# Count blocks of a graph kernel: one per pair of node blocks at fixed places, and one per tile for what runs over

## The reference

```
def _fa_layer(h, row, col, Wt_l, bt_l, Wg_l, bg_l):
    h = h @ Wt_l.T + bt_l
...
    g = jnp.tanh(h[row] @ Wg_l + bg_l)
    norm = g * dinv[row] * dinv[col]
    msg = norm[:, None] * h[row]
    out = jax.ops.segment_sum(msg, col, num_segments=n)
    return out + h
```

## Time and profile before

| | |
|---|---|
| median of three executions | 3942.78 us (3939.83 to 3947.1) |
| the profiled execution's own time | 3943.99 us |
| its span, first to last instruction | 3942.1 us |
| busy: PE, PEld | 2308.3, 2029.6 us |
| busy: DVE, ACT, POOL | 2210.6, 1280.8, 2021.6 us |
| mean granted clock of TensorE | 0.743 |

### The profile page before, as it was taken

The page is one execution under the profiler, slowest core; times in us unless marked ns, Lnnn a source line. Parts: engine busy times, 40 slices in busy tenths (PEclk is TensorE's granted clock), DMA queues, the critical chain, the costliest instruction groups (busy, mean ns, idle before and its releaser), DMA issues.

```text
span 3942.1 us, 59800 instructions
## 1 busy us (share of the span) xinstructions
PE 2308.3 (59%) x15144; PEld 2029.6 (51%) x15171; DVE 2210.6 (56%) x5804; ACT 1280.8 (32%) x3481; POOL 2021.6 (51%) x2076
## 2 busy tenths in 40 slices
PE   5972223666655666756756545554556666676665
PEld 4971213555534555545656544454445555665565
DVE  8988916777763555553665565778775222132212
ACT  4210011333220333335777754777762000000000
POOL 2777777777747777735777744777750000000000
PEclk9985555666666665556565667778778999989999
DMA  2210001122131344433333324444441222212221
GB/s 81 68 40 4 4 20 58 53 53 52 53 50 52 117 126 124 130 73 89 81 81 81 80 31 123 129 131 131 131 83 59 75 74 80 74 54 75 79 74 53
DMA packets 151496, 298.20 MB, mean 76 GB/s; under 512 B 49862, under 2 KB 67579, under 8 KB 151091
## 3 DMA queue, kind: packets, MB, share of 16 engines
q0 software_dynamic: 72704, 138.94, 15.1%
q1 hardware_dynamic: 74214, 145.16, 11.7%
q10 hardware_dynamic: 4430, 12.43, 1.0%
HBM read 249.70 MB, written 46.67 MB: 75 GB/s over the span
## 4 chain that ended last, share of the span: by engine, by line
POOL 40%; PE 24%; issue 18%; DVE 11%; ACT 3%; DMA 2%; DVEq 1%; POOLq 0%; ACTq 0%; SPq 0%
POOL arena L710 18%; PE psum L1495 15%; POOL pool L710 13%; POOL rec_dram L687 7%; DVE pool L2118 4%; PE psum L1420 3%; PE psum L1225 2%; ACT pool L882 2%; POOL ACC L710 2%; DVE ACC L2338 1%; PE psum L1263 1%; PE psum L1449 1%; ACT pool L811 1%; PE psum L1100 1%; DVE pool L1717 1%
## 5 line engine op out<-in xcount | busy, mean ns | idle before, releaser
L710 POOL DMA_INDIRECT arena<-tab_dram,tblk x832 | 794.0, 954 | 409.1 <-issue 249.5
L1495 PE MATMUL psum<-arena,pool 128*128 x4096 | 568.7, 293 | 301.3 <-DVE pool L2118 293.8
L1495 PEld LDWEIGHTS psum<-arena,pool 128*128 128x128 f32 x4096 | 527.4, 189 | 343.3 <-issue 342.7
L2118 DVE CAST pool<-pool 128x1024 f32<-128x1024 bf16 x256 | 177.1, 694 | 673.4 <-PE psum L1495 672.8
L687 POOL DMA_INDIRECT rec_dram<-arena,ACC x400 | 395.2, 988 | 196.4 <-issue 119.2
L710 POOL DMA_INDIRECT pool<-tab_dram,arena x416 | 401.1, 964 | 131.4 <-issue 126.4
L1543 PE MATMUL psum<-pool 128*128 128x136 f32 (+1 forms) x1664 | 362.0, 399 | 80.2 <-DVE pool L2262 73.9
L1543 PEld LDWEIGHTS psum<-pool 128*128 128x128 f32 x1664 | 335.3, 290 | 92.4 <-issue 51.7
L1379 PE MATMUL psum<-pool 128*128 128x128 f32 x832 | 192.8, 425 | 294.0 <-DMA pool<-tab_dram,arena 200.4
L710 POOL DMA_INDIRECT pool<-tab_dram,tblk x272 | 277.8, 1021 | 126.3 <-issue 78.6
L1379 PEld LDWEIGHTS psum<-pool 128*128 128x128 f32 x832 | 179.8, 328 | 298.4 <-DVE pool L2131 132.3
(11 more groups left out here) (378 smaller groups left out, 4760.6 us busy)
## 6 DMA issues: line engine op xcount, KB each, us to landing
pool<-items_dram SPq DMA_DIRECT2D x128, 512.0 KB, 3.3
items_dram<-pool SPq DMA_DIRECT2D x128, 256.0 KB, 2.5
pool<-dst_dram SPq DMA_DIRECT2D x104, 256.0 KB, 3.5
arena<-tab_dram,tblk POOLq DMA_INDIRECT x832
HN<-in_edge_attr_dram ACTq DMA_DIRECT2D x23, 500.0 KB
pool<-tab_dram,arena POOLq DMA_INDIRECT x416
rec_dram<-arena,ACC POOLq DMA_INDIRECT x400, 2.1
pool<-tab_dram,tblk POOLq DMA_INDIRECT x272
```

The source lines that it names most:

```text
L710: nc.gpsimd.indirect_dma_start(to[:, j, :], None, tab_dram[k], bass.IndirectOffsetOnAxis(ap=idx[:, G * g + j:G * g + j + 1], axis=0)).then ...
L1495: last = nc.tensor.matmul(psum[:, bass.ds(vals[BITE + j] * P, P)], item, of, start=False, stop=False)
L2118: v.tensor_copy(bite32[slot % 4], bite16[slot]).then_inc(s_cast, 1)
```

## The change

The items get another order and another meaning. The first FIRSTS = 640 places are one for each pair of blocks (25 x 25 = 625, then 15 of padding): place 25 d + s holds the counts of destination block d and source block s in the first tile in which that pair occurs. The remaining 416 places are one for each tile: the counts of the source block that began in an earlier tile and runs on into this one. ITEMS becomes 1056, 132 packs.

In a block pass the first kind is multiplied at addresses that are constants of the program (padding is skipped but for one matmul); the second kind still reads its block numbers, 52 times 16 of them. The order of a pass is 52 rounds of one or two packs of the first kind and one of the second, written out without a loop, on TensorE, DVE and SyncE. There are six f32 buffers instead of four. Items are stored and loaded as bytes (U8) instead of bf16, one pack (128 KB) a DMA. The tables are worked out anew for this layout; packing begins at group 8; for the second kind the picks are no products but two DVE operations over all tiles in `item_tiles`, and the picks by product are 640 wide instead of 1024.

More of the change, by code:

```diff
@@ L48 @@
 C_FIELDS, C_PICKS = 4, 8
-ROWS_THERE = 65
+ROWS_THERE = 96
+FAR = 4096.0
 BIG = 1.0e30
@@ L355, in gnn_kernel @@
[L355 to L360, removed]
@@ L362, in gnn_kernel @@
+        fields = MT[:, 1216:1216 + 3 * TILES // 2].bitcast(BF16).rearrange("p (a t) -> p a t", a=3)
+        field_i = MT[:, 1216 + 3 * TILES // 2:1216 + 5 * TILES // 2].bitcast(I32)
+        ends = [MT[:, 1216 + ITEMS * i:1216 + ITEMS * (i + 1)].bitcast(BF16).rearrange("p (w a) -> p w a", a=2) for i in range(2)]
+        behind_row = pool2[0:1, 9216:9216 + FIRSTS // 2].bitcast(BF16)
         onehots = [[ZT[:, PACK * P * b + PACK * P // 2 * e:PACK * P * b + PACK * P // 2 * (e + 1)].bitcast(BF16) for e in range(2)] for b in range(PACKS_A_GROUP)]
-        packed = [FT[:, PACK * P // 2 * b:PACK * P // 2 * (b + 1)].bitcast(BF16) for b in range(PACKS_A_GROUP)]
@@ L364, in gnn_kernel @@
-        bite16 = [pool2[:, BITE * P // 2 * b:BITE * P // 2 * (b + 1)].bitcast(BF16) for b in range(LONG)]
-        bite32 = [pool2[:, BITE * P * b:BITE * P * (b + 1)] for b in range(4, 8)]
-        where = MT[0:1, 0:2 * ITEMS].bitcast(I32)
+        packed = [FT[:, PACK * P // 4 * b:PACK * P // 4 * (b + 1)].bitcast(U8) for b in range(PACKS_A_GROUP)]
+        bite8 = [pool2[:, PACK * P // 4 * b:PACK * P // 4 * (b + 1)].bitcast(U8) for b in range(LONG)]
+        bite32 = [pool2[:, 2048 + PACK * P * b:2048 + PACK * P * (b + 1)] for b in range(HELD)]
@@ L367, in gnn_kernel @@
+        where = MT[0:1, 0:2 * TILES].bitcast(I32)
         newblk = sb("newblk", [P, 2, SLOTS * H + 1])
@@ L1474, in turn_sums, with item_regs @@
                 last.then_inc(s_itemp, 1)
-            def item_regs(n):
+            def item_regs(q):
                 _, vals = nc.values_load_multi_w_load_instructions(
-                    where[0:1, bass.ds(2 * BITE * n, 2 * BITE)], engines=[pe.engine], min_val=0, max_val=NB - 1,
+                    where[0:1, 2 * G * q:2 * G * (q + 1)], engines=[pe.engine], min_val=0, max_val=NB - 1,
                     skip_runtime_bounds_check_because="the table holds block numbers of at most NB - 1")
@@ new lines, in _ @@
+            link(v.tensor_scalar(full_, tot[:, :], 0.0, None, ALU.is_gt))
+            link(v.tensor_copy(span_i, span[:, 0, :]))
+            link(v.tensor_single_scalar(span_i, span_i, 7, ALU.arith_shift_right))
+            link(v.tensor_copy(none_, span_i))
+            link(v.scalar_tensor_tensor(none_, none_, 1.0, full_, ALU.add, ALU.mult))
+            link(v.tensor_scalar(first_tile, none_[0:NB, :], -1.0, None, ALU.add))
+            link(v.tensor_scalar(none_, full_, -1.0, -FAR, ALU.add, ALU.mult))
@@ new lines, in _ @@
+            link(v.scalar_tensor_tensor(first_behind, iota[0:NB, 0:NB], -float(P), none_[0:NB, :], ALU.mult, ALU.subtract))
+            link(v.memset(pad_tile, -1.0))
+            link(v.memset(pad_behind, -FAR))
+            for a in range(2):
+                link(v.scalar_tensor_tensor(bucket4[:, a, 0:NB], none_, FAR, span[:, a, :], ALU.mult, ALU.add))
+            link(v.tensor_scalar(bucket4[:, 2, :], iota[:, 0:28], -float(P), FAR, ALU.mult, ALU.add))
+            link(v.tensor_copy(bucket4[:, 3, :], iota[:, 0:28]))
@@ L2092, in long_pass @@
                             item_tiles()
-                        elif 4 <= g < 4 + (PAIRS + 7) // 8:
-                            for c in range(2 * g - 8, min(2 * g - 6, (PAIRS + 3) // 4)):
+                        elif 3 <= g < 3 + (PAIRS + 7) // 8:
+                            for c in range(2 * g - 6, min(2 * g - 4, (PAIRS + 3) // 4)):
                                 edge_steps(c)
```

132 lines of the change are left out of this document (55 added, 77 removed).

## The result

The changed kernel takes 3550.22 us (median of four executions, 3546.99 to 3552.29); the kernel before took 3943.23 us (four executions) on the same chip. The ratio is 0.9002, with a 95% interval of 0.8987 to 0.9018. The profiled execution took 3552.29 us around a span of 3550.4 us.

The account below looks back on a forecast made before the run. It took TensorE's sequencer, with its reads and register addresses, to bound the block passes. 870.1 - 2 x 238.5 = 393 us off, 3 on, so 390; 3943.99 - 390 - 1.2 = 3553 us, own range 3535 to 3579, 8-in-10 range 3535 to 3610.

Parts of the forecast that it names:

- The bound (the sequencer and its reads): Block passes before: TensorE's sequencer, with a 1.10 us read per bite and register work per matmul, sets the pace, not L2118.
- A pass: Each block pass after the change: 231.3 + 3.6 + 3.6 = 238.5 us, where the two took 870.1 us.
- The array's rate: TensorE's array in a block pass: 0.111 us a pair at full clock, 2084 pairs, a floor of 231.3 us.
- The missed lead: In 24 rounds with one constant-address pack, the sequencer's lead falls some 0.15 us short each: 3.6 us a pass.
- The half clock at the start: Start of a block pass: the first 64 pairs take 10.70 us instead of 7.1, costing 3.6 us.
- The 12 pairs: TensorE's sequencer can be at least 12 pairs ahead of the array, read from the start of the first block pass.
- The second sum pass: Where blocks are packed: +3 us at its end; bounds untaken were 26 us for the byte copy, 9 us back from gathers.
- Exposed loads: Rival for the block passes: no lead builds and reads stay exposed, 305 us a pass, 3686 us; chance 0.12.
- The 0.123 us a pair for register addresses: Rival: constant addresses run no faster than register ones, 263.5 us a pass, 3603 us; chance 0.06.
- The cast: Rival: DVE's cast from bytes becomes the bound, 391 us a pass, 3858 us; chance 0.05, shared with another new wait.
- Code supply: Rival: in-line passes need about 36 instruction packets; slower than before only above 10.8 us standstill each; chance 0.02.

Follow-up runs that it names:

- e7: The changed kernel with two f32 buffers for cast packs instead of six: 3553.1 us, 237.1 us a pass.
- e4: The changed kernel with the 80 constant-address packs of a pass first and the 52 register-address packs last: 3696.2 us, 308.0 us a pass.
- e6: The changed kernel with register-address packs four at a time between constant-address ones: 3649.5 us, 287.3 us a pass.
- e10: The changed kernel with a read of block numbers in every pack, kept by one register-address matmul in each constant-address pack: ratio 0.942 to before, 283.8 us a pass.
- e5: The changed kernel with register-address packs two at a time between constant-address ones: 3606.6 us, 265.0 us a pass.
- e9: The changed kernel with each register-address pack reading its 16 block numbers twice: ratio 0.939 to before, 281.0 us a pass.
- e1: The kernel before with its block passes written out in line instead of looped, all matmuls still at register addresses: 3894.5 us, 408.9 us a pass.
- e11: The changed kernel with packs 0 to 77 as matmuls of 512 columns, 4 pairs instead of 16: ratio 0.918 to before, 229.5 us a pass.
- e3: The changed kernel with a read of block numbers added to every pack, unused, so absent from the program that ran: 3553.5 us, void.

## Why the prediction was right

The prediction was 3553 us and the kernel takes 3550.2; each term against its measure:

**The bound (the sequencer and its reads).** Right. The profile's name for the wait, the cast L2118, was wrong, as argued: e7 leaves the cast a third of its buffers and the time stays, while e4 to e6 only move packs and bring back the same [<-DVE] rows. The idle column named what came last by the records it has; the sequencer's own work has no such record, and one finds it by its instructions.

**A pass.** Forecast 231.3 + 3.6 + 3.6 = 238.5; measured 235.3 and 235.8. The array's rate was sized right: 2084 x 0.1117 = 232.8 (1.5 over). The missed lead, 3.6, is nothing but the last pack's 0.4. The half clock at the start is 1.7 (3.52 us for 16 pairs instead of 1.79), not 3.6: I had it last for all 64 pairs of the row. In before it lasted for 29 of them, up to 3027.4 us, and the last 16 went at the sequencer's pace.

The step on the missed lead failed. Its 0.15 us is 1.4 for the read less 1.25 rebuilt by one constant pack; it leaves out the 0.2 us that it says the register pack lost, and the 1.25 rests on 0.033 us for handing over a constant pair, where e10 has under 0.01. So a single constant pack fills the lead up again. The 12 pairs that it took as shown, 1.34 us, were a lower bound of a row, where the bound is 16. The read and the first addresses take 1.4 us and 16 pairs last 1.79, so there is no stall. The Trainium skill (Advanced Engine Details and Errata, section Engine Queue Depths) gives TensorE a queue of 64 instructions, 32 pairs. By it too the term falls away, but the runs disagree with its figure: by 32 pairs e5 would be at 235 us a pass and e9 at 246, and they are at 265 and 281. The lead here ends at 16 pairs, 32 instructions, all of f32 matmuls.

**The second sum pass.** Forecast +3. DVE gets past the last store at 1745.71 us (L1895), and at 1743.57 in before:

```profile
1745.71 2.48 DVE L1895 TENSOR_TENSOR pool<-psum,HN 128x512 f32<-128x512 f32 x4 [14.60 <-DMA items_dram<-pool]
```

The eight profiles with the new packing where before takes 3943 to 3949 us have 1743.0 to 1747.0, mean 1745.9; the two with the old have 1743.56 and 1743.57. So +2.3. The copy to bytes costs 597 ns, as the one to bf16, and the gathers keep their 1.30 us, so neither bound of that step came into play.

**What I hadn't seen.** The block passes start 4.7 us later than in before: 2.1 from there and 2.6 from the attention stages between, which the change doesn't touch. From the end of the second sum pass to the first block pass before and e1 have 1277.7 and 1279.9 us, after 1280.3 and the seven others 1279.5 to 1283.5; whether that is more than scatter is open. Between the two block passes, from the last weight load to the first, lie 37.3 us instead of 34.7, but 34.1 to 35.2 in the seven others and 36.9 in e11, so it looks like scatter from one execution to the next. The ledger of the profiled executions by their windows: -399.0 (passes) + 4.7 (ahead) + 2.5 (between) + 0.1 (behind) = -391.7, and 3550.4 - 3942.1 = -391.7. It comes close to the 390 forecast because 6 us too much in the passes and 4 us too little ahead of and between them partly cancel.

**The rivals.** Exposed loads: not in this order, but real. It is what the same packs cost in e4, and its 305 us a pass is e4's 308. Whether it happens hangs on a margin of 0.4 to 0.6 us per register pack. The 0.123 us a pair for register addresses: L1501 follows at 1.79 us a pack, as L1505, so it belonged to the sequencer. The cast: 694 ns from bytes, as from bf16. Code supply: the instruction queue moved 34 packets more over the kernel (90 against 56; forecast were 36), and no gap in the passes answers to them; its only trace may be e1's slips, which the lead covers in after.

## What to carry to other kernels

Where TensorE has gaps and the profile names a producer that was long done, add up the sequencer's side: here 1.16 us for a read of 16 numbers, 0.245 us for each matmul at register addresses, under 0.01 us a pair at constant ones, against 0.1117 us a pair of the array. If part of the work can have constant addresses, that is not enough: it has to lie between the rest, so that each read falls into queued matmuls, and only 16 pairs count as queued, however many lie ahead. The same matmuls took 235.6 us a pass in turn, 265 by two and 308 with the register packs last.

## What the runs showed of the hardware

- Where nothing else holds TensorE's sequencer up, its lead over the array ends at 16 pairs of weight load and matmul (f32): 100 of 104 reads start at exactly 16 in after, 102 of 104 in e11. Each of them starts 0.02 us after the weight load that brings the count down to 16. At full clock 16 pairs of 128 columns are 1.79 us. In e9, 40 of 208 reads start at 17, under 0.01 us ahead of the next weight load.
- A constant pair is handed over in under 0.01 us (0.13 us for 15).
- A cast of 1024 values to f32 takes 694 ns from bytes and from bf16; a copy of 512 from PSUM takes 597 ns to bytes and to bf16.
- The rate of f32 matmuls hangs on the columns, at these two widths: 4 pairs of 512 columns take 1.72 us and 16 of 128 take 1.79.
- A read into registers that nothing uses is not in the program that runs (e3): count an experiment's instructions before its time is believed.
